# First stage of an anti-aliased leaky ReLU: slope taken apart into max(y, 0) and a linear map, row pass in 64-row tiles

## What is computed

```python
def _filtered_lrelu(x, f):          # f: 12 taps, up 2, down 2
    y = conv(x, rows up by 2);  y = conv(y, columns up by 2)
    y = where(y >= 0, y, y * 0.01)
    y = conv(y, rows down by 2);  y = conv(y, columns down by 2)
    return y
x = x + _filtered_lrelu(_gn(x), f)
x = x + _spectral_conv(_gn(x), ...)  # rfft2, 64x64 modes, a low-rank product, irfft2
```

## Time and profile before

| | us |
|---|---|
| median of 3 runs (lowest, highest) | 5322.29 (5307.2, 5323.18) |
| the profiled execution, whole time | 5309.97 |
| its span from the first to the last instruction | 5307.4 |
| PE, DVE, ACT, POOL busy in the span | 4757.2, 4019.1, 3406.9, 2960.0 |

### The profile page before, as it was taken

How to read it: one execution, slowest core, us unless ns; L and a number is a source line. 1 busy time by engine, 2 the same in 40 slices (tenths; PEclk the granted TensorE clock), 3 DMA queues, 4 the chain that set the end, 5 groups by cost and what they waited for, 6 DMA issues and landing times. The chain is left out here.

```text
span 5307.4 us, 223586 instructions
## 1 busy us (share of the span) xinstructions
PE 4757.2 (90%) x89888; PEld 4110.2 (77%) x89888; DVE 4019.1 (76%) x6181; ACT 3406.9 (64%) x6422; POOL 2960.0 (56%) x3014
## 2 busy tenths in 40 slices
PE   7898999998989999989897698898988988988999
PEld 6777777777777777777776588888888888888999
DVE  7787777777877777778776888888888888883333
ACT  6767767767677677676773566666666666663332
POOL 7868869868789689687882233333333333330000
PEclk9999999999999999999997899999999999999999
DMA  1131131131321311313214122222222222227999
GB/s 56 51 109 54 50 109 54 50 109 54 96 63 54 109 50 54 109 53 91 69 50 148 49 70 73 79 63 79 78 64 79 70 72 79 63 79 296 420 421 399
DMA packets 606643, 554.03 MB, mean 104 GB/s; under 512 B 14901, under 2 KB 540085, under 8 KB 589365
## 3 DMA queue, kind: packets, MB, share of 16 engines
q1 hardware_dynamic: 606132, 546.48, 31.3%
HBM read 277.99 MB, written 268.44 MB: 103 GB/s over the span
## 5 line engine op out<-in xcount | busy, mean ns | idle before, releaser
L1236 DVE TENSOR_TENSOR Ml<-ring,Mh 128x1024 f16<-128x1024 f32 x1024 | 1199.7, 1218 | 200.3 <-ACT Mh L1203 192.6
L285 POOL TENSOR_TENSOR Y<-Yf,Y 128x532 f16<-128x532 f32 x1024 | 1205.6, 1197 | 66.9 <-ACT Y L550 24.1
L1203 ACT ACTIVATE Mh<-ring 128x1024 f16<-128x1024 f32 x1024 | 986.6, 1022 | 301.0 <-PE ring L1137 300.5
L1137 PE MATMUL ring<-wcur,b_hi 64*128 64x128 f16 x16384 | 748.3, 217 | 176.6 <-DVE Ml L1236 137.4
L1137 PEld LDWEIGHTS ring<-wcur,b_hi 64*128 64x128 f16 x16384 | 610.2, 94 | 246.9 <-DVE Ml L1236 154.8
L713 DVE TENSOR_TENSOR Yf<-ring,L 128x532 f32<-128x532 f32 x1024 | 690.9, 709 | 125.8 <-ACT L L546 87.4
L1137 PE MATMUL ring<-wcur,b_lo 64*128 64x128 f16 x8192 | 716.0, 216 | 0.0
L328 PE MATMUL ring<-ut,g 128*128 128x266 f32 x2048 | 625.4, 430 | 60.8 <-POOL g L251 60.8
L546 ACT ACTIVATE L<-ring 128x532 f32<-128x532 f32 x1024 | 598.8, 610 | 99.8 <-PE ring L342 61.2
L693 DVE TENSOR_TENSOR A<-ring,A 128x532 f16<-128x532 f32 x512 | 364.1, 711 | 309.4 <-ACT A L537 306.7
L342 PE MATMUL ring<-uth,A 64*128 64x138 f16 x12288 | 512.3, 225 | 39.3 <-issue 27.4
(11 more groups left out here) (140 smaller groups left out, 9847.2 us busy)
## 6 DMA issues: line engine op xcount, KB each, us to landing
xb<-in_x SPq DMA_DIRECT2D x128, 512.0 KB, 4.2
x<-x1b SPq DMA_DIRECT2D x64, 1024.0 KB, 6.7
spec<-sp_out SPq DMA_DIRECT2D x256, 256.0 KB, 3.5
xin<-spec SPq DMA_DIRECT2D x128, 512.0 KB, 6.6
fd<-ft SPq DMA_DIRECT2D x128, 512.0 KB, 4.5
F<-fd SPq DMA_DIRECT2D x64, 1024.0 KB, 20.0
xq<-x SPq DMA_DIRECT2D x64, 1024.0 KB, 16.8
out<-yq SPq DMA_DIRECT2D x64, 1024.0 KB, 18.5
```

Source lines behind the costliest of these rows:

```text
L285: pool.tensor_tensor(Y[:, e, 1, m], Yf[:, m], Y[:, e, 0, m], ALU.subtract).then_inc(e_yl, 1)
L1137: mm = pe.matmul(ring[:, UNIT_PAIR[n], t, 128 * k:128 * k + 128], b[r, z, 4 * u + k, :], wcur[r, z, w, :], start=(part == 0), stop=(part = ...
L1203: act.activation(hi, ps, ACT.Copy).then_inc(e_hi, 1)
L1236: dve.tensor_tensor(lo, ps, hi, ALU.subtract).then_inc(e_lo, 1)
```

## The change

In words:

- 0.99 max(y, 0) + 0.01 y takes the place of the leaky ReLU. The factor 0.99 goes into `fac`. The part 0.01 y is linear, so its way up and down is one 128 x 128 matrix on each side, `lin`, computed once at the start (`linear_map`); its columns stand behind those of `ut`, so that `A` is 394 wide (UPA = 266 + 128). `linear_cols` adds the product into the bank of `down_cols`: 4 images x 3 products of 128 columns.
- ScalarE reads each up_cols result from PSUM as `Y` high with Relu; VectorE makes `Y` low from the same PSUM bank in one scalar_tensor_tensor (max with 0, minus high). `L`, `Lt`, `Yf`, `Ytf` are gone.
- The row pass up takes `g` as f16 high and low, in three products and in 64-row halves, each with one matmul of 138 columns and one of 69.
- ScalarE copies the row pass's result to `Af` (float32, 394 wide) and makes `g32`; GpSimd splits `Af` into `A` high and low (`split_a`), `g32` into `g` high and low (`split_g`), and the tails (`split_tail`).
- The order on TensorE is another one. Units are now U0, U1, R0, DN, TL, U2, U3, FC, R1 = 0 to 8. R1 (second half of the row pass) is unit 8 and has the same pair as TL (tails, unit 4).

The core of the diff, TensorE's step:

```diff
+            def up_rows(q, k, n, pr, swap):
+                if swap == 1:
+                    pe.wait_ge(p_rhalf, 4 * q + 2 * n + 2)
+                for part, (v, c) in enumerate(((0, 0), (0, 1), (1, 0))):
+                    for half in range(2):
+                        m = half ^ swap
+                        rows = slice(64 * half, 64 * half + 64)
+                        data = g[rows, k % 2, v, 2 * n + m, :]
+                        ups, lins = slice(128 * half, 128 * half + UPT), slice(UPS + LN0 * half, UPS + LN0 * half + LNN)
+                        pe.matmul(ring[:, pr, m, ups], data, uth[rows, c, ups],
+                                  start=(swap == 0 and part == 0), stop=False, skip_group_check=True)
+                        mm = pe.matmul(ring[:, pr, m, lins], data, uth[rows, c, lins],
+                                       start=False, stop=(swap == 1 and part == 2), skip_group_check=True)
...
+                    up_cols(q, k, 0, pr[U0], 0)
+                    wait(pe, e_yl, 4 * q)
+                    free(2)
+                    up_cols(q, k, 1, pr[U1], 0)
+                if nxt:
+                    pe.wait_ge(e_gl, q + 2)
+                    wait(pe, e_x1, q - 1)
+                    wait(pe, e_g, q - 2)
+                    free(3)
+                    up_rows(q + 1, k + 1, 0, pr[R0], 0)
                 if up:
+                    up_cols(q, k, 0, pr[U0], 1)
+                    up_cols(q, k, 1, pr[U1], 1)
+                if nxt:
+                    up_rows(q + 1, k + 1, 0, pr[R0], 1)
...
+                    down_rows(q, o, pr[DN])
...
+                    tails(e, o, pr[TL], up, down)
+                if up:
+                    pe.wait_ge(e_al, 2 * q + 2)
+                    pe.wait_ge(e_yl, 4 * q + 2)
+                    up_cols(q, k, 2, pr[U2], 0)
...
+                    up_cols(q, k, 3, pr[U3], 0)
                 if nxt:
+                    pe.wait_ge(e_ytl, q + 1)
                     if down:
                         pe.wait_ge(e_ztl, q)
+                    up_rows(q + 1, k + 1, 1, pr[R1], 0)
+                if up:
+                    up_cols(q, k, 2, pr[U2], 1)
+                    up_cols(q, k, 3, pr[U3], 1)
+                if nxt:
+                    up_rows(q + 1, k + 1, 1, pr[R1], 1)
```

More of the change, by code:

```diff
@@ L14 @@
+import math
 from contextlib import ExitStack, contextmanager
@@ L270, in variance, with step @@
                 pool.tensor_scalar(var[:], var[:], 0.0, 2 * EPS, ALU.max, ALU.add).then_inc(k_var, 1)
[L272 to L291, removed]
+            def step(q, k, nxt=True, half=None, ground=True):
                 if half is not None and k % HALF == 2:
                     variance(half)
[L294 to L298, removed]
+                if nxt:
+                    split_a(q + 1, k + 1, 0)
+                if ground:
+                    split_g(q + 2, k + 2)
+                if nxt:
+                    split_tail(q + 1, k + 1)
+                    split_a(q + 1, k + 1, 1)
             def first():
@@ new lines, in up_cols @@
+            def up_cols(q, k, m, pr, swap):
+                if swap == 1:
+                    pe.wait_ge(p_half, 8 * q + 2 * m + 2)
+                for part, (v, c) in enumerate(((0, 0), (0, 1), (1, 0))):
+                    for half in range(2):
+                        t = half ^ swap
+                        rows, cols = slice(64 * half, 64 * half + 64), slice(128 * half, 128 * half + UPT)
+                        mm = pe.matmul(ring[:, pr, t, cols], A[rows, k % 4, v, m, 128 * t:128 * t + 128],
+                                       uth[rows, c, cols], start=(swap == 0 and part == 0),
+                                       stop=(swap == 1 and part == 2), skip_group_check=True)
+                        if part == 2:
+                            mm.then_inc(p_s2 if swap else p_half, 1)
@@ L400, in step, with free @@
                 e, o = k % 2, 1 - k % 2
                 pr = [pair_of(k, u) for u in range(9)]
-                def row_transform():
-                    pe.wait_ge(e_x1, q - 1)
-                    for m in range(IMGS):
-                        mm = pe.matmul(ring[:, pr[8], 1, 128 * m:128 * m + 128], x1b[:, (k - 2) % SLOTS, m, :],
-                                       dfth[:], start=True, stop=True)
-                    mm.then_inc(p_s5, 1)
+                def free(units):
+                    if after is not None:
+                        pe.wait_ge(e_s6, UNITS6 * after + 12 + units)
@@ L456, in step @@
+                if nxt:
+                    up_rows(q + 1, k + 1, 1, pr[R1], 1)
                 if down:
                     pe.wait_ge(e_zl, q)
-                    pe.wait_ge(e_ztl, q)
-                    if not up:
-                        pe.wait_ge(e_yf, 4 * NQ)
-                    down_cols(o, pr[8])
-                if rows and batch is None:
-                    row_transform()
+                if rows:
+                    pe.wait_ge(e_x1, q - 1)
+                    for m in range(IMGS):
+                        mm = pe.matmul(ring[:, pr[FC], 1, 128 * m:128 * m + 128], x1b[:, (k - 2) % SLOTS, m, :],
+                                       dfth[:], start=True, stop=True)
+                    mm.then_inc(p_s5, 1)
@@ L465, in spectra @@
+                if down:
+                    linear_cols(k - 1, pr[FC])
+                    down_cols(o, pr[FC])
+                    pe.wait_ge(e_ztl, q)
+                    down_cols_tail(o, pr[FC])
             def spectra(b, q):
```

406 lines of the change are left out of this document (204 added, 202 removed).

## The result

The changed kernel takes 5616.15 us (median of 4 runs, 5611.68 to 5618.24), the kernel before 5320.74 beside it: a ratio of 1.056, 95% interval 1.054 to 1.0579. The change makes it slower, by 295 us where 645 were forecast; the time lies at the very lower end of the stated range of 5600 to 6250. The profiled executions stand 306 us apart (spans 5613.4 and 5307.4). The sign and the place were right; the size was not, and most of this document is about which terms were too large.

The account below looks back on a forecast made before the run. TensorE was taken to set the pace, GpSimd close behind. Work and stalls, 9.10 + 1.87 + 0.64 = 11.61 us a step against 9.59, gave +512 over 256 steps on 5310; with +133 for the clock, 5955 us, range 5600 to 6250.

Parts of the forecast that it names:

- TensorE's own work: TensorE's matmuls per step: 8.69 less 0.60 (row pass) plus 0.75 (linear_cols) plus a rest of 0.26, 9.10 us.
- the clock: Phase 1: one R1 stall in two brings half clock at 1.43 us, 183 us, less 50 paid today: net +133.
- R1's stall: TensorE before R1 waits for Yt low and Zt low: 1.87 us a step, bounds 1.6 and 2.0.
- the count of steps: The step's growth of 2.02 us was multiplied by 256 steps: +517 us, rounded to +512.
- R0's stall: TensorE before R0 waits for x1b, sharing FC's pair: 0.64 us a step, bounds 0.4 and 0.8.
- rival 6: Both stalls at or under their lower bounds, clock as now: 10.93 us a step, some 5650 down to 5600; chance 0.07.
- The rule on order: Row pass: if matmuls start in program order, a half quad takes 0.91 us, not 0.75, and the sum is 82 us higher.
- rival 2: The clock falls at nearly each stall: 6138 us; chance 0.10.
- rival 4: The 64-row row pass gets no overlap: 1.36 us each, +1.22 a step, 6267 us; chance 0.06.
- rival 3: Faster: no stalls at R1 and R0, step is TensorE's work alone, 9.10 us, 5185 in all; chance 0.07.
- rival 5: GpSimd becomes the bound through costlier 788-element forms, beyond 11.6 us a step, near 6050; chance 0.03.
- rival 1: The clock holds as today despite the stalls: 5822 us; chance 0.25.

Follow-up runs that it names:

- e3: Changed kernel with VectorE making Z low twice, the first time into a tile nobody reads, ahead of R1: 6107.02 us.
- e12: Changed kernel with VectorE making Zt low twice, the first time into a tile nobody reads, ahead of R1: 5725.77 us.
- e1: Changed kernel with R1 moved back behind the second swaps of U2 and U3: 5517.17 us.
- e2: Changed kernel with all of R1 moved behind the second swaps of U2 and U3 and the row transform: 5453.29 us.
- e5: Changed kernel with both swaps of R0 moved behind the second swaps of U0 and U1: 5578.92 us.
- e8: Changed kernel with the edits of e2 and e5 together: 5403.77 us.
- e6: Changed kernel without the 12 matmuls of linear_cols, so 0.01 y is missing from the result: 5601.09 us.
- e7: Changed kernel in e4's order, but statistics' sums behind tails, row transform between U2/U3 and R1, both swaps of each together: 5299.6 us.
- e10: Changed kernel with the edits of e9 and e6 together (g32 earlier, no linear_cols): 5599.32 us.
- e4: Changed kernel, units reordered: U0, U1, down_rows, sums, tails, R0, row transform, linear_cols, down_cols, then U2, U3, R1; ScalarE and VectorE work moved too: 5553.49 us.
- e9: Changed kernel with ScalarE making g32 ahead of Y high 2 and 3 in three of four steps: 5602.25 us.
- e11: e7 with ScalarE making g32 behind the second Af in each fourth step: 5405.5 us.

## Why the prediction was right in sign and too high

**The place and the cause: right, shown.** TensorE stands before R1 with Zt low as the releaser (379.6 us in 254 waits, one in each step). Lengthening VectorE's chain lengthens the plain step one to one (e3, e12), moving R1 and R0 shortens it (e1, e2, e5, e8), leaving out arithmetic doesn't (e6), and another order with all the arithmetic isn't slower than before (e7). By the Trainium skill (TensorEngine Tiling (Array Packing), PSUM Bottleneck), tiling speeds up TensorE but not the evacuation of PSUM. The trace agrees: the two row passes fell from 2.10 to 1.32 us a step, while the readers Z high and Z low take 1.02 and 1.22 us each in both kernels. That the time saved came back as 2.2 us of waits is the order's doing, though: e7 keeps the tiled row pass, and has no wait before R1.

**What failed** is the sum "+2.02 a step, over 256 steps, and one stall in two at half clock", in four of its terms, none of them much larger than the others: TensorE's own work (8.84 us assumed, 8.39 measured, some 98 us in all), the clock (183 less 50 us assumed, about 38 measured, 95 us), R1's stall taken as alike in every step (1.87 against a mean of 1.49, 82 us), and the count of steps (256 taken; 39 of them, at loops' and batches' ends, grew by next to nothing, 70 us). The last two had no reason beside them: I never asked in which steps other work or another wait fills the same time.

**The size: 339 us too much** (645 against 306). By terms:

- **R1's stall, 1.87 forecast, 1.49 the mean** (379.6 / 254). The chain was 2.99 us (1529.75 to 1532.74) and not 3.17, since Yt low and Zt low overlap and the release took 0.14 and not 0.25; TensorE had 1.36 and not 1.27. That gives 1.63, near the lower bound. And in each fourth step the sums stand before R1: I had put them into the rest of 0.26 and not asked where they lie. 0.38 a step.
- **R0's stall, 0.64 forecast, 0.68 the mean** (at this line in phase 1: 120.1 us for g, 6.3 for x1b, 29.5 without a releaser, in 228 waits). The mean is right by luck: the plain step has 0.52, and the fourth 1.13, for new statistics that I hadn't looked at. The releaser is half wrong: g low and x1b end together, and I named x1b alone. I had costed GpSimd "at nothing", as busy 7.7 us of a step (7.4 measured, 1888.5 / 256); but its work on g hangs on ScalarE's g behind Y high 3, and a chain can be late on an engine that is idle a third of the time.
- **TensorE's own work, 8.84 without the rest of 0.26, measured 8.39** (the plain step's 10.54 less 1.63 and 0.52 of idle time; 8.42 of 10.60 us busy in the stretch above). By medians from start to start in phase 1: a row pass half quad took 0.27 + 0.39 = 0.66 us and not 0.75; linear_cols 0.67 (1534.76 to 1535.43) and not 0.75; the row transform behind a row pass 1.00 and not 1.09; down_cols, whose last matmuls overlap the next block, 0.84 and not 1.00. The largest of these is the row pass, and e7 says why: there its two swaps stand side by side and the second waits for the first, and the same half quad takes 0.93 to 0.95. In after an up_cols stands between them and covers that wait. I had weighed three rates for the columns and not the place of the block. 0.45 a step. (The 9.10 of the prediction is more than the 8.95 of before, not "hardly less"; measured, the work did fall.)
- **The loop's end.** I multiplied by 256. But in the 32 steps at a loop's end the change costs 0.25 us (387.9 us in all before, 396.0 after): TensorE already stood there for "issue" while the readers caught up. The seven steps with a batch end are alike (some 42 us each in both kernels). 39 steps, 70 us too much.
- **The clock: +133 forecast, about +38.** The other 217 steps grew 1.16 us at the full clock, 252 us; together with the batch ends they grew 290; the rest, 38, is the clock's. I took one stall in two; 74 stretches in 256 steps is fewer than one in three, and they cost 1.4 us each, as taken. 95 us too much. (Counting stretches gives another split: 44 more than before, at 1.4 us, are 62 us. The line between step and clock is no sharper than that.)
- The start, left out, took 10 us more (first Z high of phase 1 at 46 us, before at 36).

The first three make 0.38 - 0.04 + 0.45 = 0.79 us of the 0.86 by which the step was over (2.02 against 1.16); 0.07 is left for the ends between blocks. 0.86 x 217 = 187 us; 187 + 70 + 95 - 10 = 342, less 5 of my rounding: 337 of the 339.

Every one of these but R0's leaned the same way. I took the stall near its upper bound, the rate for the clock from two lengths of stall with one or two cases each, and the whole number of steps; the lower ends together were rival 6, which I gave 0.07, and the measured time lies there. Its time was right (5650 and down to 5600), its chance was not, and part of the hit is luck: it keeps TensorE's work at 8.93 and the stalls at 2.0 in all 256 steps, where the steps came out with less work, stalls of 2.2, 39 steps that hardly grew, and a lower clock.

Of the signs that the prediction named, the stall before R1 with Zt low as the releaser came true (1.63 us for some 1.9). Steps are 10.54 to 11.15 us where 11 to 12 were named, the clock of phase 1 is 0.96 and not near 0.9, and in the fourth step the longest wait is the one for g (1.13 against 1.09), which was named as a sign of being wrong.

**The rule on order.** The 24 matmuls of a row pass half quad take 0.66 us, about what their columns ask (the 0.68 of the prediction). That they don't start in the order of the code shows in the first of them (TensorE, after), and in the same way in 1008 of the 1024 groups of twelve:

```profile
1503.41 0.24 PE L345 MATMUL ring<-uth,g 64*128 64x138 f16 x2 [0.65 <-POOL g L253]
1503.47 0.21 PE L347 MATMUL ring<-uth,g 64*128 64x69 f16 x2
1503.50 0.24 PE L345 MATMUL ring<-uth,g 64*128 64x138 f16 x2
```

The code alternates L345 and L347, first for one half of the rows, then for the other. The trace shows two L345 (one for each half), then two L347: the long matmul of the second half starts 0.05 us before the short one of the first, which stands ahead of it. By the Trainium skill (TensorE: Matmul & The Clock Gate, Part 3) matmuls start and end in program order. The trace contradicts it for the starts of two row halves (the ends it shows are modelled), and the 0.91 us that followed from it was wrong.

**The other rivals.** The clock falling at nearly each stall (rival 2): only e3, with a stall of 2.8 us, came near it, 216 in 256. A row pass without overlap (rival 4): no, 0.66. Faster (rival 3): the point from which it decides, both stalls under 0.49, was far off: they are 2.2. GpSimd as the bound (rival 5): its 788-element forms take 1.68 + 0.84 us, under the 1.77 + 0.93 assumed. The clock unchanged (rival 1): no, but nearer than one in two.

**What stays open.** Why the stalls without a releaser ("issue") at a loop's end change with the order; the changed kernel has 15% more TensorE instructions and its instruction queue moved 512 packets for 411, but no run varied the loop alone. Why e10 and e6, whose stalls before R1 are as in after, have more half-clock stretches (123 and 106 for 74): 37 and 36 of them begin in the fourth step, where after has 11, and there a wait of 0.3 us for Y low has joined those before R1 and R0; that this is the cause is not shown. And an order that keeps the interleaved swaps (8.39 us of work in a plain step, e7 9.08) without e4's waits was not built.

## What to carry to other kernels

When an order is written by hand, count for each PSUM buffer the work between its last reader's start and its next writer, not the busy shares: here the same arithmetic was 5.6% slower than the kernel before in one order and level with it (0.3% under) in another. Cost a stall by the step in which other work fills it as well (here the sums once in four steps, loop ends and batch ends), and not by the number of steps alone; and ask of each duration that is copied from a trace what waits inside it. Before one stall is removed, find the branches that end within a few tenths of it, for they take its place: e4, e6, e9, e10 and e11 each removed one link and met the next.

## What the hardware showed that was not expected

- **The clock fell more often the longer the stall before R1, and steeply.** With some 11 us from step to step, and nearly all else as in after, a stall of 1.2 us gave 17 half-clock stretches in 256 steps (e1), 1.63 us gave 74 (after), 1.83 gave 114 (e12), 2.8 gave 216 (e3). Between the first two, 0.4 us of stall moved phase 1's mean clock from 0.99 to 0.96 and the time by 99 us, of which the step itself explains 16. So here the last tenths of a stall were worth more than their length. This one stall isn't all that counts: e6 and e10 have 106 and 123 stretches with the same 1.63 us, and e2, whose plain step has no stall over 0.57, has 35, of which 13 begin in its fourth step, behind a wait for g of 1.3 us.
- **Two matmuls of the two row halves pass one another**, as shown above: two 64-row streams with unequal columns (138 and 69) take 0.66 us for 24 matmuls, in proportion to the columns of up_cols (0.68).
- **The wait between two swaps is worth 0.3 us.** The second pass into the same banks waits for the first. Side by side, the two swaps of a row pass half quad took 0.93 to 0.95 us (e7), with an up_cols between them 0.66. For up_cols the same shows: one swap of two images with a row pass on either side took 0.36, so 0.72 for both, where the two swaps as one block take 0.90.
